# An adaLN block on one Trainium2 core: layer-norm rows of three batches on GpSimd, and one gated product over two PSUM banks

## The chip, the core and the metric

The kernel runs on one core of one Trainium2 chip, on float32 data, in one launch. A core has four engines that compute (TensorE, here PE; VectorE, DVE; ScalarE, ACT; GpSimd, POOL) and SyncE (SP), which issues transfers. Each takes its own instructions in order; they meet by semaphores. The metric is the device time in microseconds (us); less is better.

## What is computed

For x of 4 batches x 1024 rows x 128 columns, with a modulation `mod = silu(c) @ wmod` that gives each batch six vectors (sa, ca, ga, sb, cb, gb):

```python
h = layernorm(x) * (1 + ca) + sa
q, k = l2norm(heads(h @ Wq)), l2norm(heads(h @ Wk)); v = heads(h @ Wv)      # 16 heads of 8
...   # beta, two decays, a per-token gate "flux" from a tiny MLP on k*beta
M_fast, M_slow = einsum(k * beta * w, v * beta) / w.sum()                   # over all 1024 rows
x = x + ga * ((alpha * q @ M_fast + (1 - alpha) * q @ M_slow) @ Wo)
h = layernorm(x) * (1 + cb) + sb
x = x + gb * fp4_linear(silu(fp4_linear(h, w_gate)) * fp4_linear(h, w_up), w_down)   # 352 hidden columns
```

`fp4_linear` rounds activations and weights to a four-bit grid, with one scale for each block of 16 columns, before it multiplies. ga and gb are kept at least 0.25 away from zero.

## The kernel before

The rows of a batch lie as 8 tiles of 128 rows; the unit of work is a pair of tiles, so there are 16 pairs, four to a batch (pair i is of batch i // 4). Everything is fully unrolled. What each engine does in which order is written out by hand in the table ORDER, one list for each engine, of steps like `PP:5` (step PP of pair 5) or `GA:1` (step GA of batch 1); each engine's block walks its list and runs the step's function, if it has one. Waits are on counters whose values follow from these lists. Nothing else sets the order of the work.

Phase one, for each batch. P0 (DVE L797 to L805) takes mean and variance of the 8 tiles, POOL turns the variance into `rstd` with a power (L385). XN makes the normalised tile `xn` = (x - mean) * rstd: for batches 0 and 1 on VectorE (L751, one TENSOR_SCALAR a tile), for batches 2 and 3 on ScalarE (L567, one ACTIVATE a tile, which needs nmr = -mean * rstd, made on POOL, L389). XN_VECTOR = 2 is that border. `xn` has four tiles, two pairs, so XN of pair i waits for the transposes of pair i - 2. PX transposes a pair on TensorE (L1063, L1064) into a bank; ScalarE moves it out as `hT` with the modulation applied (L576). PP multiplies hT by all of the projection weights (L1074, 496 columns a tile); ScalarE copies keys, values and gates to `kvg` (L589) and squares queries and keys to `sq` (L592), and VectorE sums the squares (L810). MB makes the modulation matrices `mb` from wmod (PE, ACT L541), and W0 on VectorE (L779 to L789) brings their gates to the right sign and size.

Then the gate steps of a batch, a long chain over all engines: GA (ACT: table load L512, exp, ln; VectorE's part is zb L824 and, as GB, eg1 L832), GC (POOL adds the logs L405, PE sums them over rows), GD (ACT wexp L624), GS (ACT hmid L633), GE, GF, GY, and V0 to V3 (POOL L424 makes the weighted values, PE L1095 multiplies them with the keys), GG (the memory matrix `wm`). O1, O2 and O3 read the memory for a pair, transpose, and multiply by Wo; O3 on VectorE adds the result to x and takes new statistics. L1 normalises again (ACT L664, POOL L448, L452).

Phase two quantises. A slot s serves the normalised rows of pair s - 4 and the gated FFN rows of pair s - 6 at once, 960 columns: Q (DVE L934 maximum, L939, L942 reciprocal), QR (POOL L461), QA (ACT L675), QT (DVE L950, L953), QO (POOL L473). N4 transposes the first part. F1 multiplies it by the gate and up weights: tile 0's G0 and U0, then tile 1's G1 and U1 (PE L1148, L1150), 352 columns each; G goes to the `pa` banks, U to the `pv` banks. ScalarE makes silu of G0 and G1 to `sgl` (L690), VectorE multiplies each with its U bank into q_x (L964). F3 transposes the quantised products, F4 multiplies by the down weights on top of x, and the pair goes out.

PSUM: three `pa` banks are handed round among all users of that kind (the position in the PE list decides), two `pv` banks among O1, O3 and F1, so a pair's U0 can be in either of the two. `sgl` has two tiles: silu of tile k waits until the product of the pair before has read it.

Transfers are issued by SyncE in this order: x of batch 0 (two halves), the first third of wmod, Wv, three gate weights, x of batch 1, the rest of wmod (L310), five small vectors, Wo, five pieces of the FFN weights, x of batches 2 and 3 (L325). ScalarE issues c, Wtf1, Wk and Wq.

Of the kernel before, what the change touches and what calls it, by code (L numbers as in the profile page):

```python
# [11 lines left out]
P = 128  # L12
# [73 lines left out]
        Q:21 QT:20 QT:21""",
    "tensor": """
        CT:0 RP:0 CM:0 WK:0 WQ:0 PX:0 PX:1 KW:0 PX:2 PP:0 PX:3 PP:1 PX:4 PP:2 PX:5 PP:3 PX:6 MB:0 PX:7 PP:4 PP:5
        PP:6 PX:8 PX:9 GC:0 PX:10 PP:7 PP:8 PP:9 PX:11 GE:0 PP:10 V0:0 V1:0 V2:0 V3:0 PP:11 GG:0 GC:1 O1:0 O1:1
        GE:1 O2:0 PX:12 O2:1 O1:2 O3:0 PX:13 PP:12 O2:2 O3:1 O1:3 V0:1 V1:1 V2:1 V3:1 PX:14 O3:2 O2:3 PP:13 GG:1  # L90
        GC:2 O3:3 W3:0 GE:2 O1:4 O1:5 N4:0 PX:15 PP:14 PP:15 F1:0 O2:4 V0:2 O2:5 O3:4 V1:2 O1:6 V2:2 N4:1 V3:2
        O3:5 F1:1 N4:2 F3:0 F1:2 O2:6 GG:2 F4:0 O3:6 O1:7 GC:3 O1:8 N4:3 F1:3 O2:7 O2:8 GE:3 F3:1 O1:9 N4:4 F1:4
        O3:7 V0:3 O2:9 V1:3 F3:2 O3:8 V2:3 F4:1 N4:5 F1:5 V3:3 F3:3 O1:10 N4:6 O3:9 F4:2 F1:6 F3:4 O2:10 GG:3
        O1:11 O1:12 O3:10 N4:7 O2:11 F4:3 O3:11 F1:7 N4:8 F1:8 F4:4 F3:5 O1:13 O2:12 F3:6 O1:14 O3:12 O2:13 N4:9
        F1:9 O2:14 F4:5 O3:13 F3:7 O3:14 F4:6 N4:10 O1:15 F1:10 N4:11 F1:11 F3:8 O2:15 F4:7 O3:15 F3:9 F4:8
        N4:12 F3:10 F1:12 N4:13 F1:13 F3:11 F4:9 F4:10 F4:11 N4:14 F1:14 N4:15 F1:15 F3:12 F3:13 F4:12 F4:13
# [1109 lines left out]
```

## Time and profile before

| | us |
|---|---|
| three timed runs: median (lowest to highest) | 219.83 (219.64 to 221.18) |
| the profiled execution, by the same clock | 217.84 |
| its span from first to last instruction | 216.0 |
| VectorE / ScalarE / GpSimd busy in the span | 177.0 / 148.3 / 148.0 |
| TensorE matmuls busy | 182.3 |

A time in the trace counts from the start of the span. The profile is of one execution, whose time is the second line; the timed runs are others. Line numbers (L964) are those of the kernel before; names such as `q_x<-sgl,pv` are out<-in; x8 is a number of instructions; "idle before" or square brackets tell how long the engine stood before them and who let it go on.

### The profile page before, as it was taken

The page shows a single profiled execution, that of the slowest core. Times are in us where ns is not written, and L with a number is a line of the kernel's source. Part 1 is how long each engine was busy: PE and PEld are TensorE (multiplying, and loading weights), DVE is VectorE, ACT ScalarE, POOL GpSimd, SP SyncE. Part 2 cuts the span into 40 slices and gives each one's busy share as a digit, 9 for nine tenths or more (in the row PEclk, how much of TensorE's full clock was granted, in tenths as well). Part 3 has the DMA queues.
Part 4 walks back from the last instruction along what each step waited for, and adds up shares of the span by engine and source line. Part 5 has one row for each costly group of instructions (what it writes and reads, how often), then busy time and mean ns, then how long its engine had stood idle before and what let it go on. Part 6 is the DMA issues. An engine that isn't in the chain of part 4 may idle for free. (4 is left out here: it accounts for less than half of the span.)

```text
span 216.0 us, 3457 instructions
## 1 busy us (share of the span) xinstructions
PE 182.3 (84%) x924; PEld 131.0 (61%) x924; DVE 177.0 (82%) x444; ACT 148.3 (69%) x342; POOL 148.0 (68%) x174
## 2 busy tenths in 40 slices
PE   1996935699999989788599999889899898988983
PEld 1642414256767737656375868767688595775863
DVE  3959989756899979899999999998999996876730
ACT  2486997999999997964973656464844557563641
POOL 6334007674879978898978997877858768765540
PEclk9999995999999999999999999999999999999999
DMA  5591000000000000000000010000001000011011
GB/s 163 165 257 35 0 2 0 0 3 0 2 2 0 5 0 0 0 0 5 0 24 0 0 27 26 0 27 3 24 0 49 3 24 24 6 41 32 0 52 49
DMA packets 11500, 5.66 MB, mean 26 GB/s; under 512 B 1685, under 2 KB 11353, under 8 KB 11481
## 3 DMA queue, kind: packets, MB, share of 16 engines
q1 hardware_dynamic: 11168, 5.31, 8.8%
q8 instruction: 8, 0.13, 0.3%
q10 hardware_dynamic: 312, 0.13, 0.2%
q14 instruction: 12, 0.09, 0.1%
HBM read 3.34 MB, written 2.10 MB: 25 GB/s over the span
## 5 line engine op out<-in xcount | busy, mean ns | idle before, releaser
L461 POOL TENSOR_TENSOR q_r<-q_x,q_rs 128x960 f32<-128x960 f32 (+2 forms) x18 | 29.7, 1651 | 13.4 <-DVE q_rs L942 13.4
L473 POOL TENSOR_TENSOR q_o<-q_r,q_sp 128x960 f32<-128x960 f32 (+2 forms) x18 | 29.5, 1641 | 8.8 <-DVE q_r L953 8.3
L1074 PE MATMUL pa<-wcat,hT 128*128 128x496 f32 x64 | 31.3, 615 | 3.0 <-ACT hT L576 1.7
L1148 PE MATMUL pa<-guT,hqT 128*128 128x352 f32 x64 | 25.2, 476 | 5.6 <-ACT hqT L681 5.6
L675 ACT ACTIVATE q_A<-q_r 128x960 f32<-128x960 bf16 (+2 forms) x18 | 16.0, 887 | 16.3 <-POOL q_r L461 11.1
L1171 PE MATMUL pa<-wdg,fqT 128*128 128x128 f32 x192 | 26.7, 275 | 0.0
L690 ACT ACTIVATE sgl<-pa 128x352 f32<-128x352 f32 x32 | 14.6, 462 | 15.5 <-PE pa L1148 12.6
L1150 PE MATMUL pv<-guT,hqT 128*128 128x352 f32 x64 | 24.3, 461 | 0.0
L1171 PEld LDWEIGHTS pa<-wdg,fqT 128*128 128x128 f32 x192 | 24.0, 192 | 0.0
L424 POOL TENSOR_TENSOR vs<-kvg,cw 128x256 f32<-128x256 f32 x32 | 20.0, 649 | 3.8 <-DVE cw L848 3.8
L1074 PEld LDWEIGHTS pa<-wcat,hT 128*128 128x128 f32 x64 | 11.4, 200 | 16.0 <-ACT sq L592 6.0
L950 DVE SCALAR_TENSOR_TENSOR q_x<-q_A,q_r 128x960 f32<-128x960 f32 (+2 forms) x18 | 18.5, 1026 | 2.8 <-ACT q_A L675 2.8
L964 DVE TENSOR_TENSOR q_x<-sgl,pv 128x352 f32<-128x352 f32 x32 | 15.7, 510 | 6.0 <-PE pv L1150 5.5
L934 DVE TENSOR_REDUCE q_am<-q_x 128x60 f32<-128x960 f32 (+2 forms) x18 | 18.7, 1040 | 1.0 <-POOL q_x L452 0.5
L953 DVE SCALAR_TENSOR_TENSOR q_r<-q_A,q_x 128x960 f32<-128x960 f32 (+2 forms) x18 | 18.8, 1046 | 0.6
L1148 PEld LDWEIGHTS pa<-guT,hqT 128*128 128x128 f32 x64 | 11.0, 189 | 11.8 <-ACT hqT L681 7.8
L405 POOL TENSOR_TENSOR lf<-lf 128x224 f32<-128x224 f32 (+2 forms) x12 | 8.2, 680 | 13.3 <-ACT lf L616 12.7
L1150 PEld LDWEIGHTS pv<-guT,hqT 128*128 128x128 f32 x64 | 12.0, 190 | 7.2 <-DVE x_all L905 0.8
L589 ACT ACTIVATE kvg<-pa 128x368 f32<-128x368 f32 x32 | 15.3, 479 | 1.5 <-PE pa L1074 1.3
L1112 PE MATMUL pv<-wm,hT 128*128 128x256 f32 x64 | 16.1, 382 | 0.2 <-DVE x_all L905 0.2
L698 ACT ACTIVATE fqT<-pa 128x384 f32<-128x384 f32 x32 | 14.0, 487 | 3.2 <-PE pa L1159 3.1
L664 ACT ACTIVATE xn<-x_all,nmrb,rstdb 128x128 f32<-128x128 f32 x32 | 14.0, 489 | 2.6 <-DVE nmrb L923 2.6
(151 smaller groups left out, 449.8 us busy)
## 6 DMA issues: line engine op xcount, KB each, us to landing
out_dram<-x_all SPq DMA_DIRECT2D x16, 128.0 KB, 1.8
x_all<-in_L_attn_x_dram SPq DMA_DIRECT2D x3, 512.0 KB, 5.6
x_all<-in_L_attn_x_dram SPq DMA_DIRECT2D x2, 256.0 KB, 3.1
wmod_sb<-in_L_wmod_dram SPq DMA_DIRECT2D x1, 256.0 KB, 4.3
wraw<-in_L_ffn_w_down_dram SPq DMA_DIRECT2D x1, 176.0 KB, 4.2
wmod_sb<-in_L_wmod_dram SPq DMA_DIRECT2D x1, 128.0 KB, 3.8
wraw<-in_L_ffn_w_gate_dram SPq DMA_DIRECT2D x1, 128.0 KB, 3.6
wraw<-in_L_ffn_w_up_dram SPq DMA_DIRECT2D x1, 128.0 KB, 3.1
```

The costliest lines, as they stand in the source:

```text
L424: g.tensor_tensor(vs[:, t].rearrange("p a (h d) -> p a h d", d=DK), vt.unsqueeze(1).to_broadcast([P, 2, H, DK]), cw[:, t].unsqueeze(3).to_ ...
L461: g.tensor_tensor(blocks(q_r[:, s % 2, c]), blocks(q_x[:, s % 2, c]), spread(q_rs[:, s % 2, n]), ALU.mult)\
L473: g.tensor_tensor(blocks(q_o[:, s % 2, c]), blocks(q_r[:, s % 2, c]), spread(q_sp[:, s % 2, n]), ALU.mult)\
L675: a.activation(q_A[:, c], top, ACT.Abs, scale=TOP_SCALE).then_inc(S["q_A"], 1)
L934: v.tensor_reduce(q_am[:, r, n], blocks(q_x[:, r, c]), axis=AX.X, op=ALU.max, apply_absolute_value=True)\
L950: v.scalar_tensor_tensor(q_x[:, r, c], q_A[:, c], MAGIC_FLOOR, q_r[:, r, c], ALU.max, ALU.add)\
L953: v.scalar_tensor_tensor(q_r[:, r, c], q_A[:, c], MAGIC_FLOOR, q_x[:, r, c], ALU.max, ALU.subtract, reverse1=True).then_inc(S["q_q"], 1)
L1074: te.matmul(bank_a(("PP%d" % k, i))[:, 0:NCAT], hT[:, b, 2 * j + k, :], wcat[:, :], start=True, stop=True).then_inc(S["a_full"], 1)
L1112: last = te.matmul(t[:, k * 2 * D:(k + 1) * 2 * D], hT[:, b, 2 * j + k, :], wm[:, b % 2, :], start=True, stop=True)
L1148: te.matmul(bank_a(("G%d" % k, i))[:, 0:I], lhs, guT[:, 0, :], start=True, stop=True)\
L1150: te.matmul(bank_v(("U%d" % k, i))[:, 0:I], lhs, guT[:, 1, :], start=True, stop=True)\
L1171: last = te.matmul(t[:, k * D:(k + 1) * D], fqT[:, (2 * i + k) % 4, ch * P:(ch + 1) * P], wdg[:, b % 2, ch, :], start=False, stop=(ch == 2))
```

## The change

XN moves: batch 0 stays on VectorE, batches 1, 2 and 3 go to GpSimd, as TENSOR_SCALARs with mean and rstd as per-partition scalars; nmr is no longer made. `sgl` becomes two pairs of tiles. The two `pv` banks are one tensor, so that VectorE multiplies both tiles of a pair in one instruction of 2 x 352 columns, after silu of G1 and after U1; it frees both banks at once. TensorE still makes G0, U, G1, U, but which tile's U comes first depends on the bank, so that tile 0 always lies in bank 0. x of batch 2 is issued before the rest of wmod, x of batch 3 last. All four lists of ORDER are written anew.

```diff
-    XN_VECTOR = 2
+    XN_ON = "vggg"
...
-        sgl = sb("sgl", [P, 2, I])
+        sgl = sb("sgl", [P, 2, 2, I])
...
-        pv = [ctx.enter_context(nc.psum_tensor(f"pv{i}", [P, 512], F32)) for i in range(NBANK_V)]
+        pv_all = ctx.enter_context(nc.psum_tensor("pv", [P, NBANK_V, 512], F32))
+        pv = [pv_all[:, k, :] for k in range(NBANK_V)]
...
# SyncE
-            sp.dma_start(wmod_sb[:, 2 * D:6 * D], wmod[:, 2 * D:6 * D]).then_inc(S["wmod"], 16)
...
             sp.dma_start(btf2_b[:, :], btf2.partition_broadcast(P)).then_inc(S["wsm"], 16)
+            sp.dma_start(x_all[:, 2], x_v[2]).then_inc(S["x2"], 16)
+            sp.dma_start(wmod_sb[:, 2 * D:6 * D], wmod[:, 2 * D:6 * D]).then_inc(S["wmod"], 16)
             sp.dma_start(wo_sb[:, :], Wo).then_inc(S["wo"], 16)
...
-            for b in range(2, NB):
-                sp.dma_start(x_all[:, b], x_v[b]).then_inc(S["x%d" % b], 16)
+            sp.dma_start(x_all[:, 3], x_v[3]).then_inc(S["x3"], 16)
# GpSimd
+            def XN(i):
+                b, j = divmod(i, NP_)
+                if XN_ON[b] != "g":
+                    return
+                pool.wait_ge(S["nmean"], stat_count(b, 0))
+                pool.wait_ge(S["rstd"], stat_count(b, 0))
+                if i >= 2:
+                    pool.wait_ge(S["a_full"], slot_a[("XT", i - 2)] + 1)
+                for k in range(2):
+                    t = 2 * j + k
+                    g.tensor_scalar(xn[:, t % 4, :], x_all[:, b, t, :], nmean[:, b, t:t + 1], rstd[:, b, t:t + 1],
+                                    ALU.add, ALU.mult).then_inc(S["xnp"], 1)
# ScalarE, F1
+                if i >= 2:
+                    act.wait_ge(S["v_free"], slot_v[("U1", i - 2)] + 1)
                 for k in range(2):
                     t = bank(("G%d" % k, i))
-                    n = 2 * i + k
-                    if n >= 2:
-                        act.wait_ge(S["v_free"], slot_v[("U%d" % k, i - 1)] + 1)
-                    a.activation(sgl[:, n % 2, :], t[:, 0:I], ACT.Silu).then_inc(S["a_free"], 1)
+                    a.activation(sgl[:, i % 2, k, :], t[:, 0:I], ACT.Silu).then_inc(S["a_free"], 1)
# VectorE, F1
-                for k in range(2):
-                    n = 2 * i + k
-                    t = bank(("U%d" % k, i))
-                    dve.wait_ge(S["a_free"], slot_a[("G%d" % k, i)] + 1)
-                    v.tensor_tensor(q_x[:, r, k * I:(k + 1) * I], sgl[:, n % 2, :], t[:, 0:I], ALU.mult)\
-                        .then_inc(S["v_free"], 1)
+                bank(("U0", i))
+                bank(("U1", i))
+                dve.wait_ge(S["a_free"], slot_a[("G1", i)] + 1)
+                v.tensor_tensor(q_x[:, r, 0:2 * I].rearrange("p (t k) -> p t k", t=2), sgl[:, i % 2], pv_all[:, :, 0:I],
+                                ALU.mult).then_inc(S["v_free"], 2)
# TensorE, F1
+                first = slot_v[("U0", i)] % NBANK_V
...
+                    t = k ^ first
+                    te.matmul(bank_v(("U%d" % k, i))[:, 0:I], hqT[:, i % 2, t * D:(t + 1) * D], guT[:, 1, :],
+                              start=True, stop=True).then_inc(S["v_full"], 1)
```

Of the lists, the stretches around the first gate block. Before and after:

```diff
 scalar
-  ... PX:5 PP:3 PX:6 XN:8 MB:0 PX:7 XN:9 PP:4 PP:5 GA:0 PP:6 PX:8 XN:10 PX:9 W1:0 GD:0 GS:0 PX:10 PP:7 ...
+  ... PP:3 PX:5 MB:0 PX:6 PP:4 WQ:0 PX:7 GA:0 PP:5 PP:6 PX:8 W1:0 PX:9 GD:0 GS:0 PP:7 PP:8 PX:10 ...
 vector
-  ... P0:1 XN:3 XN:4 PP:0 XN:5 XN:6 P0:2 PP:1 PP:2 XN:7 GA:0 PP:3 P0:3 W0:0 GB:0 ...
+  ... XN:3 P0:1 PP:0 P0:2 PP:1 PP:2 GA:0 PP:3 P0:3 W0:0 GB:0 ...
 gpsimd
-  P0:0 P0:1 P0:2 KC:0 GC:0 GB:0 V0:0 V1:0 P0:3 V2:0 GF:0 V3:0 GC:1 ...
+  P0:0 P0:1 XN:4 XN:5 XN:6 P0:2 KC:0 XN:7 P0:3 GO:0 XN:8 XN:9 GC:0 GB:0 XN:10 GO:1 V0:0 XN:11 V1:0 V2:0 V3:0 XN:12 GF:0 GC:1 GB:1 W2:0 XN:13 XN:14 ...
```

From F1:0 on the lists hold the same steps as before with small exchanges of neighbours.

## Rows read from the trace of the kernel before

**Rows 1.** Busy time by stage: length, PE, PEld, DVE, ACT, POOL busy, granted clock, DMA.

```profile
0.00:20.00 20.00, 13.46 (x42) 7.54 (x43) 13.66 (x79) 10.85 (x29) 8.33 (x17) 1.00 0.62 168
20.00:41.00 21.00, 14.06 (x36) 6.68 (x35) 18.56 (x46) 19.24 (x43) 7.38 (x16) 0.84 0.00 0
41.00:82.00 41.00, 38.78 (x163) 26.01 (x164) 33.11 (x93) 39.93 (x106) 32.40 (x48) 1.00 0.01 1
82.00:180.00 98.00, 86.76 (x503) 67.81 (x501) 91.95 (x200) 61.19 (x130) 81.32 (x82) 1.00 0.04 12
180.00:216.00 36.00, 29.22 (x186) 22.91 (x183) 19.77 (x30) 17.05 (x39) 18.55 (x15) 1.00 0.11 31
```

**Rows 2.** Waits (us in total, times, longest), TensorE 41 to 82, ScalarE 20 to 82.

```profile
PE pa L1074 <- ACT hT L576: 1.7, 1, 1.7
...
ACT wexp L624 <- PE pg L1083: 1.2, 1, 1.2
```

**Rows 3.** Groups by line: ScalarE's XN in all, in 41 to 82 us, VectorE's XN.

```profile
L567 ACT ACTIVATE xn<-x_all,nmr,rstd 128x128 f32<-128x128 f32 x16 | 7.0, 496 | 0.2 <-POOL nmr L389 0.2
...
L567 ACT ACTIVATE xn<-x_all,nmr,rstd 128x128 f32<-128x128 f32 x10 | 4.4, 496 | 0.0
...
L751 DVE TENSOR_SCALAR xn<-x_all,nmean,rstd 128x128 f32<-128x128 f32 x16 | 4.6, 341 | 1.3 <-issue 1.3
```

**Rows 4.** Groups by line, GpSimd.

```profile
L385 POOL TENSOR_TENSOR rstd<-ve,mhalf 128x8 f32<-128x8 f32 x3 | 5.2, 1722 | 9.4 <-DVE ve L804 9.4
...
L434 POOL TENSOR_TENSOR wog<-wo_sb,mb 128x128 f32<-128x128 f32 x4 | 1.8, 460 | 0.0
...
L357 POOL TENSOR_SCALAR w_s<-w_sp 128x70 f32<-128x70 f32 x1 | 0.3, 261 | 0.1
```

**Rows 5.** Timeline (start, us): SyncE's issues, VectorE and ScalarE at batch 2's arrival.

```profile
4.73 0.58 SPq L310 DMA_DIRECT2D wmod_sb<-in_L_wmod_dram  x1
...
10.65 1.36 SPq L325 DMA_DIRECT2D x_all<-in_L_attn_x_dram  x2
...
16.22 1.64 DVE L797 BATCH_NORM_STATS2 st<-x_all 128x6 f32<-128x128 f32 x8 [1.31 <-DMA x_all<-in_L_attn_x_dram]
...
19.31 0.38 ACT L592 ACTIVATE sq<-pa 128x256 f32<-128x256 f32 x1 [1.70 <-DVE ss L810]
```

**Rows 6.** Timeline from 28 to 34 us: VectorE, then ScalarE behind GA:0.

```profile
28.41 0.69 DVE L789 SCALAR_TENSOR_TENSOR mb<-mb_sgn,mb 128x512 f32<-128x512 f32 x1
29.80 0.36 DVE L832 TENSOR_SCALAR eg<-eg 128x384 f32<-128x384 f32 x1 [0.70 <-ACT eg L601]
...
32.03 0.46 ACT L589 ACTIVATE kvg<-pa 128x368 f32<-128x368 f32 x1
...
33.27 0.59 ACT L576 ACTIVATE hT<-pa,colmod 128x256 f32<-128x256 f32 x1
```

**Rows 7.** Timeline, VectorE: the gated products and a 704-column operation.

```profile
117.30 0.52 DVE L964 TENSOR_TENSOR q_x<-sgl,pv 128x352 f32<-128x352 f32 x1 [0.30 <-PE pv L1150]
...
145.13 0.95 DVE L964 TENSOR_TENSOR q_x<-sgl,pv 128x352 f32<-128x352 f32 x2
146.12 1.15 DVE L934 TENSOR_REDUCE q_am<-q_x 128x60 f32<-128x960 f32 x1
...
200.80 0.52 DVE L964 TENSOR_TENSOR q_x<-sgl,pv 128x352 f32<-128x352 f32 x1 [0.61 <-PE pv L1150]
...
202.84 0.83 DVE L950 SCALAR_TENSOR_TENSOR q_x<-q_A,q_r 128x704 f32<-128x704 f32 x1
203.70 0.89 DVE L953 SCALAR_TENSOR_TENSOR q_r<-q_A,q_x 128x704 f32<-128x704 f32 x1
```

**Rows 8.** VectorE's coefficient row: duration ns minimum/median/maximum.

```profile
L877 DVE SCALAR_TENSOR_TENSOR coef<-yt,rn x4: 279/284/1229, 49.7 to 132.8; 128x128 f32<-128x128 f32 x4
```

**Rows 9.** The chain that ended last (start, us, what), two of its pieces.

```profile
172.80 0.53 DVE q_x L964
...
203.01 1.38 POOL q_r L461
```

More of the change, by code:

```diff
@@ L87 @@
[L87 to L96 removed]
+        P0:0 P0:1 XN:4 XN:5 XN:6 P0:2 KC:0 XN:7 P0:3 GO:0 XN:8 XN:9 GC:0 GB:0 XN:10 GO:1 V0:0 XN:11 V1:0 V2:0
@@ new lines @@
+        QR:19 QO:18 QO:19 GH:3 QR:20 QR:21 QO:20 QO:21""",
+    "scalar": """
+        CT:0 CM:0 WK:0 PX:0 PX:1 PX:2 KW:0 PX:3 PP:0 PP:1 PP:2 PX:4 PP:3 PX:5 MB:0 PX:6 PP:4 WQ:0 PX:7 GA:0 PP:5
+        PP:6 PX:8 W1:0 PX:9 GD:0 GS:0 PP:7 PP:8 PX:10 GE:0 PP:9 PX:11 GA:1 PP:10 PP:11 GG:0 GD:1 GS:1 O2:0 PX:12
+        O2:1 PP:12 O2:2 GE:1 GA:2 L1:0 PX:13 O2:3 PX:14 L1:1 PP:13 GD:2 W3:0 QA:4 GG:1 GS:2 N4:0 QA:5 PX:15
+        PP:14 L1:2 PP:15 F1:0 L1:3 O2:4 O2:5 GA:3 QA:6 N4:1 F1:1 GE:2 L1:4 N4:2 F1:2 GS:3 O2:6 QA:7 GG:2 F3:0
+        GD:3 QA:8 F4:0 L1:5 N4:3 F1:3 O2:7 O2:8 L1:6 F3:1 N4:4 F1:4 GE:3 QA:9 F3:2 QA:10 F4:1 O2:9 N4:5 L1:7
+        F1:5 F3:3 N4:6 QA:11 L1:8 F1:6 F4:2 O2:10 GG:3 F3:4 QA:12 L1:9 O2:11 N4:7 F4:3 L1:10 F1:7 N4:8 F1:8 F3:5
+        O2:12 QA:13 F3:6 QA:14 F4:4 O2:13 N4:9 L1:11 F1:9 O2:14 L1:12 F4:5 QA:15 N4:10 F4:6 F3:7 L1:13 F1:10
+        N4:11 F1:11 O2:15 QA:16 F4:7 F3:8 QA:17 F3:9 F4:8 L1:14 N4:12 F1:12 N4:13 L1:15 F1:13 F3:10 QA:18 F4:9
+        F3:11 QA:19 F4:10 F4:11 N4:14 F1:14 N4:15 F1:15 F3:12 QA:20 F3:13 F4:12 QA:21 F4:13 F3:14 F4:14 F3:15
+        F4:15""",
@@ L265, in adaln_block_kernel @@
                 "xn2", "u", "wdg", "c", "wqk", "w1", "btf2h", "w_r", "w_A", "xn", "col", "zb", "kvg", "ss",
-                "eg1", "eg", "lnss", "rn", "lg", "hz", "al0", "yt", "nmrb", "bias0", "scB", "xn0", "w_rs",
+                "eg1", "eg", "lnss", "rn", "lg", "hz", "al0", "yt", "nmrb", "bias0", "scB", "xn0", "xnp", "w_rs",
                 "w_t", "bn", "mv", "nmean", "cf", "rt", "rt1", "mrt", "sfx", "coef", "bnb", "mvb", "eps", "h2", "w_sp", "x1",
@@ L290, in stat_count, with xn_nth @@
             return k + 1 if b == 0 else b + 2
+        def xn_nth(i):
+            return sum(1 for k in range(i + 1) if XN_ON[k // NP_] == XN_ON[i // NP_])
         def gates(b, lo, hi):
@@ L483, in GH @@
                                 ALU.mult).then_inc(S["wdg"], 1)
-            run = {"KC": KC, "W2": W2, "W3": W3, "P0": P0, "GB": GB, "GC": GC, "GF": GF, "GO": GO, "GH": GH, "O3": O3, "L1": L1,
+            run = {"KC": KC, "XN": XN, "W2": W2, "W3": W3, "P0": P0, "GB": GB, "GC": GC, "GF": GF, "GO": GO, "GH": GH, "O3": O3, "L1": L1,
                    "QR": QR, "QO": QO}
@@ L559, in XN @@
                 b, j = divmod(i, NP_)
-                if b < XN_VECTOR:
+                if XN_ON[b] != "a":
                     return
-                act.wait_ge(S["nmr"], b - XN_VECTOR + 1)
+                act.wait_ge(S["nmr"], XN_ON[:b + 1].count("a"))
                 if i >= 2:
@@ L742, in XN @@
                 b, j = divmod(i, NP_)
-                if b >= XN_VECTOR:
+                if XN_ON[b] != "v":
                     return
```

61 lines of the change are left out of this document (26 added, 35 removed).

## Prediction

> **What bounds the kernel now.** I read the busy time by stage first. From 20 to 82 us ScalarE (ACT) has hardly a free moment (59.2 of 62 us; in 41 to 82 us 39.9 of 41), with TensorE just below it in the second part (38.8 of 41). From 82 to 180 us VectorE is the full engine (92.0 of 98), GpSimd (POOL) has 81.3 and ACT only 61.2. In the last 36 us nobody is full: quantise, transpose and multiply of the last pairs follow each other [rows 1]. The waits say the same: between 41 and 82 us TensorE's projection waits for ScalarE to turn a transposed tile into hT (the longest wait 1.7 us), while ScalarE's own longest wait between 20 and 82 us is 1.2 us, for the sum over the decays [rows 2]. So up to the first FFN product (F1:0, at the border of these stages, 82 us) the time is ScalarE's, behind it VectorE's, and the end is a chain.
>
> **Part 1: the layer-norm rows of batches 1 to 3 go to GpSimd.** ScalarE loses 16 ACTIVATEs of 496 ns, which occupy it for 7.0 us because neighbours overlap; 10 of them, 4.4 us, lie between 41 and 82 us and the other six, 2.6 us, before. VectorE loses 8 of its 16 rows, half of 4.6 us = 2.3 us [rows 3]. GpSimd gets 24 TENSOR_SCALARs 128x128 with one tensor input and two per-partition scalars. The trace has no such row. The nearest from below is a TENSOR_SCALAR 128x70 of 261 ns, from above a two-input TENSOR_TENSOR 128x128 of 460 ns, and very far off the 8-element power, 1722 ns, whose cost is its function and not its length [rows 4]. I take 0.35 us, nearer to the one-input row: 24 x 0.35 = 8.4 us (6.3 to 11.0 by the two near ends, 41 by the far one). GpSimd has 11.7 + 13.6 = 25.3 us free before 41 us and 8.6 us in 41 to 82 [rows 1]; some 14 of the 24 run in the first part and 10 in the second (3.5 us), so at 0.35 us they hide under its own idle time. Without that cover each would delay GpSimd's next step by its length. The Trainium skill ("GPSIMD Engine Reference", section Engine selection) says that one-input work on GpSimd runs at roughly line rate and two-input work at half of VectorE's; by its cycle figure 128 elements take about 0.11 us beside the dispatch, an estimate that would put the row at the lower end; the 261 ns row, one-input too, agrees in kind, and no row here has the two scalars.
>
> **Part 2: transfers.** x of batch 2 is issued at 10.65 us, behind the rest of wmod, wo and five FFN weight transfers. VectorE, which takes its queue in order, stood 1.31 us for it at 16.2 us; the sum of squares behind it came late, and ScalarE stood 1.70 us for that at 19.3 us [rows 5]. Twelve issues lie between 4.73 us (wmod) and 10.65 us, 0.49 us each [rows 5]. In the new order seven of those ahead of it come behind, so batch 2 is issued and lands some 3.4 us earlier and the stall goes: -1.7 us. What could be late next: wmod is issued 2.9 us later, at about 7.7 us, but its matrices (MB) are made only after the stalled ScalarE step of 19.3 us, so it is not; batch 3 comes last as before and is read after batch 2's and four pairs' work.
>
> **What it gives by stage.** The first gate block of batch 0 (GA:0) does not become free by what ScalarE loses: in the middle of it, eg1 on VectorE runs at 29.80 us behind the modulation's sign steps, whose last starts at 28.41 and takes 0.69 us [rows 6], and these wait for the matrices. It moves by the 1.7 us of the stall. From there to 41 us ScalarE loses the pair XN:10 (2 x 0.44 = 0.9 us) and, since work is moved in ahead of the decay step, its 1.2 us of waiting [rows 2], and gets the pair PP:5 that stood ahead of GA:0 (33.27 - 32.03 = 1.24 us) [rows 6]: -0.9. That makes -2.6 us at 41 us. TensorE has only 14.1 of 21 us of work there and a mean granted clock of 0.84, part of the stretch at the lower level of 1.2 GHz, against 1.00 after it [rows 1]; GA:0 still blocks ScalarE in the same way, so I leave that as it is. From 41 to 82 us ScalarE would give 4.4 us, but TensorE has only 41.0 - 38.8 = 2.2 us to lose [rows 1], and three rotating banks will not close all of it. I take 1.5 us, between 0 and 4.4. So F1:0 comes 4.1 us earlier. VectorE behind it is as full as before with the same list of work, so the shift is kept to the end; the 2.3 us of its own rows lie before 21 us, where it is busy 13.7 of 20 us anyway [rows 1].
>
> **Part 3: one product for two tiles.** Two instructions of 352 columns, back to back, keep VectorE for 146.12 - 145.13 = 0.99 us. For 704 columns with one operand in PSUM the nearest is L950 to L953 at the end, 203.70 - 202.84 = 0.86 us. So a pair whose inputs are all there gains 0.13 us. But where VectorE waits for the second up-projection it is the other way: before, 0.52 us were left once U1 had ended (start 117.30), now the whole 0.88 us start there: +0.36. Such a second product with a gap of its own, 0.3 to 0.6 us, appears seven times in 16, first at 117.30 and last at 200.80 [rows 7]. All in all 9 x -0.13 + 7 x 0.36 = +1.3 us if each counted. The chain that ended last passes the product of 172.80 (late one), and ends over q_r at 203.01 [rows 9], which waits for the reciprocal behind the product of 200.80 (late one); a third product on it is back to back. That is 2 x 0.36 - 0.13 = +0.6 us, which I take; ends -16 x 0.13 = -2.1 and 7 x 0.36 = +2.5. Both banks now come free together, half a microsecond later for the first; TensorE's next user of it stands behind other matmuls mostly, so I add nothing. The silu rows get a full second buffer and lose no time. The Trainium skill ("VectorE: DVE Perf Modes", Rules for kernel authors) advises fewer VectorE operations since each pays its start; its figure of about 150 cycles (156 ns) would give 16 x 0.156 = -2.5 us as an estimate. The rows show 0.13 instead, and only where nothing is awaited.
>
> **Sum.** -2.6 - 1.5 + 0.6 = -3.5 us. Against the profiled execution (217.84 us, span 216.0) that is 214.3; the median of the three timed runs is 2.0 us higher, 219.83, so the forecast for it is **216.3 us**. The new written order on every engine can move each of these terms by a microsecond.
>
> **Rivals.**
> A. ScalarE alone was the limit, TensorE only looked full because its rows follow ScalarE's pace: the full 7.0 us and the 1.7 us stall come back, with no loss in the product: 219.8 - 8.7 = 211.1 us. For it: ScalarE's 1.1 us of idle in 41 us. Against: TensorE has 2.2 us of idle there, and its matmuls do not get shorter.
> B. TensorE holds the second stage and the late products all count: -2.6 + 0 + 2.5 = -0.1: 219.7 us, no change. For it: the 38.8 of 41 us and the seven gaps. Against: most gaps lie where VectorE is not on the chain.
> C. Slower. GpSimd's queue is in order, and each XN waits there for a transpose two pairs earlier, with GC, V and QR behind it. Its room in 41 to 82 us is 8.6 us; ten rows fill it at 0.86 us each, and from there every further tenth costs 1 us. At the far end (1.72 us) it is 17.2 - 8.6 = +8.6 us, less the 2.6 of before: 219.8 + 6.0 = 225.8 us. For it: per-partition scalars on GpSimd are not in the trace. Against: the 261 ns row. Waits for the transposes work alike: XN:8 also stands behind GO:0, which waits for the sign steps ending at 29.1 us.
> D. The two engines get in each other's way. A coefficient row on VectorE takes 279 ns at least and 1229 at most [rows 8], so something now and then holds it for 0.95 us. If half of the 24 new rows hold a VectorE step for their own 0.35 us while it is full (18.6 of 21 us, [rows 1]), that costs 4.2 us, of which the idle time hides half: 216.3 + 2.1 = 218.4 us. The Trainium skill ("SBUF — State Buffer", Who interferes with whom) says that GpSimd and a VectorE operation with two SBUF inputs exclude each other for a whole instruction; by that rule the spread of that row is such a lock, and the trace agrees in that it occurs.
>
> **How the numbers follow.** Forecast 0.45, A 0.20, B 0.15, C 0.10, D 0.10. A measurement of this kernel tells about 1% from no change, 2.2 us, so faster means below 217.6. Of the forecast's 0.45 (its own range 213.5 to 218.5) 0.39 lies below that, all of A, and a little of D: 0.61. B, most of D and the rest of the forecast: 0.27. C and the tail of B: 0.12. The range reaches from A (211.1) to beyond B: 211.0 to 220.6, leaving out most of C and a little at the low end.
>
> **What the profile after would show.** GpSimd's new row at 0.3 to 0.45 us, 24 times; no ACTIVATE from x_all and nmr; no wait for x at 16 us; eg1 of batch 0 near 28.1; the first gated product 4 us earlier than before; ScalarE below 37 of 41 us in the second stage with TensorE at 38 or more; one product of 0.85 to 0.9 us, 16 times; VectorE's stage from F1:0 to the tail as long as before or up to 1 us longer. I am wrong if the row costs over 0.8 us, if F1:0 moves by 7 us or not at all, or if the stretch behind F1:0 changes by more than 2 us.

## The result, and the profile after

The changed kernel takes 223.09 us (median, 221.1 to 224.57) against 219.85 us for the kernel before in the same rounds: a ratio of 1.013, 95% interval [1.0095, 1.0165]. It is slower by 1.3%, 2.1 to 3.6 us. The medians are of all executions, while the ratio leaves out those that were over 1.5% above the fastest of their kernel (four of the ten after, near 224.5 us). The profiled execution took 221.18 us (span 219.4); for the kernel before those were 217.84 and 216.0. Single profiles are read here for where time goes, the ratios for how much.

Busy time by stage of the kernel after, same columns as in [rows 1] (the last stage ends at 219.4):

```profile
0.00:20.00 20.00, 14.67 (x39) 7.78 (x40) 12.03 (x73) 10.52 (x27) 10.79 (x23) 1.00 0.62 168
20.00:41.00 21.00, 16.11 (x43) 7.42 (x42) 19.52 (x46) 19.15 (x42) 15.20 (x26) 0.92 0.00 1
41.00:82.00 41.00, 39.08 (x170) 26.67 (x170) 34.29 (x93) 37.62 (x95) 36.57 (x58) 1.00 0.00 1
82.00:180.00 98.00, 86.32 (x488) 66.89 (x487) 87.43 (x179) 57.65 (x122) 76.83 (x78) 0.98 0.04 12
```

Up to 82 us the picture is near the predicted one: from 41 us on ScalarE has 37.6 of 41 us where it had 39.9 (I had said below 37), TensorE is at 39.1, and GpSimd works 26.0 of the first 41 us where it worked 15.7: the new rows lie in what was its idle time. From 82 us on VectorE, the engine that was full before (92.0 of 98), is busy only 87.4: it now waits. The product's group before, then after (line, engine, operation, count | busy us, mean ns | idle before and who ended it):

```profile
L964 DVE TENSOR_TENSOR q_x<-sgl,pv 128x352 f32<-128x352 f32 x32 | 15.7, 510 | 6.0 <-PE pv L1150 5.5 <-issue 0.3
```

```profile
L980 DVE TENSOR_TENSOR q_x<-sgl,pv 128x704 f32<-128x704 f32 x16 | 14.1, 884 | 12.2 <-PE pv L1164 11.1
```

The new rows on GpSimd, first as a group, then with the minimum, median and maximum duration in ns:

```profile
L406 POOL TENSOR_SCALAR xn<-x_all,nmean,rstd 128x128 f32<-128x128 f32 x24 | 12.2, 516 | 2.8 <-DVE nmean L822 2.5 <-issue 0.2 <-PE pa L1077 0.2
```

```profile
L406 POOL TENSOR_SCALAR xn<-x_all,nmean,rstd x24: 441/447/1582, 13.6 to 72.8; 128x128 f32<-128x128 f32 x24
```

The product's group had 6.0 us of idle ahead of it before and has 12.2 now. The new GpSimd row takes 447 ns in the median, where I had taken 0.35 us. Some rows take longer, so the mean is 516 ns and the whole step 12.2 us, beyond the upper of my two near ends (6.3 to 11.0). The longest, 1.58 us, is the second of a pair, beside a row of VectorE with 1120 columns and two inputs in SBUF:

```profile
35.33 2.01 POOL L406 TENSOR_SCALAR xn<-x_all,nmean,rstd 128x128 f32<-128x128 f32 x2
```

```profile
35.76 1.34 DVE L787 SCALAR_TENSOR_TENSOR wraw<-w_A,w_r 128x1120 f32<-128x1120 bf16 x1 [0.79 <-ACT w_A L563]
```

So the two engines seem to have got in each other's way here too, at the rows where rival D had looked.

Where the time went is best read by single events that both kernels have. The starts of the first silu of F1:0 on ScalarE, before and after:

```profile
81.85 0.47 ACT L690 ACTIVATE sgl<-pa 128x352 f32<-128x352 f32 x1
```

```profile
79.72 0.52 ACT L707 ACTIVATE sgl<-pa 128x352 f32<-128x352 f32 x1
```

So F1:0 comes 2.1 us earlier, not 4.1. The end of the first product moves by less, 84.5 to 83.0. The ends of the gated products of pairs 0 to 15, taken off VectorE's timeline of each kernel (us; the experiments are explained below):

| kernel | 0 | 1 | 2 | 3 | 4 | 5 | 9 | 12 | 15 |
|---|---|---|---|---|---|---|---|---|---|
| before | 84.5 | 94.8 | 99.5 | 112.7 | 117.8 | 128.2 | 160.0 | 184.0 | 201.3 |
| after | 83.0 | 93.5 | 99.8 | 112.0 | 118.2 | 129.0 | 161.8 | 186.8 | 204.7 |
| after, exchange undone (n13) | 82.4 | 92.9 | 97.3 | 109.9 | 115.6 | 126.4 | 159.1 | 184.2 | 202.1 |
| after, split products (m2) | 84.9 | 95.2 | 101.6 | 114.0 | 119.2 | 131.5 | 163.2 | 187.2 | 205.1 |
| both undone (n14) | 83.2 | 93.5 | 98.1 | 110.6 | 115.7 | 126.4 | 158.2 | 182.1 | 200.0 |
| best (m6) | 82.5 | 92.8 | 97.5 | 110.7 | 115.8 | 126.2 | 158.0 | 182.0 | 199.3 |
| best with merged product (m11) | 81.8 | 92.4 | 97.5 | 112.4 | 118.2 | 129.4 | 162.2 | 187.3 | 204.9 |
| best with the exchange (n16) | 82.1 | 92.4 | 98.8 | 111.0 | 116.1 | 126.5 | 158.3 | 182.3 | 199.6 |

Each row is one execution, with its own stretches at the lower clock: m2's has one from 40 to 48 us (mean granted clock 0.78), where n14's has none, and m2 is 1.7 us later from product 0 on. Differences within a row say more than those between rows.

Two losses show behind the earlier start. One is sudden: from product 1 to product 2 the kernel after takes 6.3 us where before took 4.7, and its lead of 1.3 us is gone (it has 0.7 of it once more at product 3, and is behind from product 4 on). The other is a drift: from product 4 to 15 it takes 86.5 us where before took 83.5.

The sudden one can be seen in the timelines. The kernel before, then after (start, duration, engine, line, operation):

```profile
98.07 0.53 DVE L942 RECIPROCAL q_rs<-q_sp 128x60 f32<-128x60 f32 x1
98.52 0.10 DVE L923 SCALAR_TENSOR_TENSOR nmrb<-mvb,rstdb 128x2 f32<-128x2 f32 x1
98.53 0.94 DVE L964 TENSOR_TENSOR q_x<-sgl,pv 128x352 f32<-128x352 f32 x2
...
98.68 1.82 POOL L461 TENSOR_TENSOR q_r<-q_x,q_rs 128x960 f32<-128x960 f32 x1 [0.86 <-DVE q_rs L942]
```

```profile
96.60 0.53 DVE L959 RECIPROCAL q_rs<-q_sp 128x60 f32<-128x60 f32 x1
97.04 0.36 DVE L902 TENSOR_TENSOR mbd<-pg,mrt 128x256 f32<-128x256 f32 x1
97.32 1.72 DVE L940 SCALAR_TENSOR_TENSOR nmrb<-mvb,rstdb 128x2 f32<-128x2 f32 x1
98.97 0.87 DVE L980 TENSOR_TENSOR q_x<-sgl,pv 128x704 f32<-128x704 f32 x1
...
97.20 1.82 POOL L479 TENSOR_TENSOR q_r<-q_x,q_rs 128x960 f32<-128x960 f32 x1 [0.69 <-DVE q_rs L959]
```

nmrb has two elements a partition and takes 0.10 us before and 1.72 us after. It ends at 99.04, and GpSimd's q_r at 99.02. Both engines wait for the same reciprocal. Before, nmrb follows the reciprocal at once and starts 0.16 us ahead of q_r; after, one of the "small exchanges of neighbours" (`GG:2 Q:7` has become `Q:7 GG:2`) has put the mbd row of GG:2, 0.36 us, between them, nmrb starts 0.12 us behind q_r and stays until q_r is done. And it is on the chain that ended last (pieces in order of time, the kernel after):

```profile
97.05 0.05 DVE mbd L902
97.10 0.22 issue
97.32 1.72 DVE nmrb L940
99.05 0.81 DVE q_x L980
99.85 0.14 issue
99.99 2.04 PE pv L1125 x4
```

The four matmuls behind it take 2.04 us; in the kernel with the exchange undone (n13, below) the same four take 1.10. TensorE had stood 1.83 us for this product, whose bank they need, and its granted clock was at the lower level in part of the next stretch (windows of the kernel after, columns as in [rows 1]):

```profile
96.00:100.00 4.00, 1.75 (x10) 0.88 (x8) 3.93 (x6) 3.33 (x8) 3.23 (x4) 0.95 0.00 0
100.00:104.00 4.00, 4.00 (x16) 3.48 (x17) 3.90 (x6) 1.32 (x4) 2.59 (x3) 0.62 0.00 0
```

A mean of 0.62 over 4 us, between levels 1.0 and 0.5, is about 3 us at 1.2 GHz. The Trainium skill ("SBUF — State Buffer", Who interferes with whom) says that GpSimd and a VectorE operation with two SBUF inputs shut each other out for a whole instruction. The trace agrees: the held row reads mvb and rstdb, both in SBUF. In the kernel before, the products behind nmrb, each with one operand in PSUM, took their usual 0.94 us for two beside the running q_r (98.68 to 100.50).

### The profile page after: what moved, and what is told of

It reads as the page before. It is cut to its first block, busy times and chain, and to the rows that moved or that the text cites. A ratio compares the mean times of both kernels' runs of the same rounds, so it can differ in the third digit from the quotient of the medians.

```text
span 219.4 us, 3421 instructions
## 1 busy us (share of the span) xinstructions
PE 186.3 (85%) x924; PEld 132.3 (60%) x924; DVE 175.4 (80%) x420; ACT 144.4 (66%) x326; POOL 160.3 (73%) x196
## 4 chain that ended last, share of the span: by engine, by line
PE 31%; DVE 18%; POOL 17%; ACT 16%; issue 16%; DMA 1%; DVEq 0%; POOLq 0%; ACTq 0%
PE pa L1087 6%; POOL q_r L479 5%; PE pa L1161 5%; POOL q_o L491 4%; PE pv L1164 4%; ACT L530 4%; PE pa L1185 3%; ACT hmid L651 2%; DVE q_x L967 2%; DVE q_x L980 2%; POOL q_x L466 2%; DVE hz L873 2%; PE pv L1125 2%; PE pa L1173 2%; DVE ss L827 2%
## 5 line engine op out<-in xcount | busy, mean ns | idle before, releaser
L479 POOL TENSOR_TENSOR q_r<-q_x,q_rs 128x960 f32<-128x960 f32 (+2 forms) x18 | 29.7, 1651 | 17.2 <-DVE q_rs L959 16.3
L1087 PE MATMUL pa<-wcat,hT 128*128 128x496 f32 x64 | 33.0, 641 | 5.3 <-ACT sq L610 5.1
L980 DVE TENSOR_TENSOR q_x<-sgl,pv 128x704 f32<-128x704 f32 x16 | 14.1, 884 | 12.2 <-PE pv L1164 11.1
L1087 PEld LDWEIGHTS pa<-wcat,hT 128*128 128x128 f32 x64 | 12.0, 206 | 18.2 <-ACT sq L610 9.1
L1125 PE MATMUL pv<-wm,hT 128*128 128x256 f32 x64 | 17.5, 402 | 2.3 <-DVE q_x L980 1.8
L466 POOL TENSOR_TENSOR q_x<-xn,mb 128x256 f32<-128x256 f32 x16 | 11.6, 726 | 6.6 <-issue 6.6
L1108 PE MATMUL pg<-vs,kvg 128*128 128x256 f32 x64 | 15.9, 381 | 0.6 <-DVE ws L878 0.6
```

The costliest lines, as they stand in the source:

```text
L479: g.tensor_tensor(blocks(q_r[:, s % 2, c]), blocks(q_x[:, s % 2, c]), spread(q_rs[:, s % 2, n]), ALU.mult)\
L980: v.tensor_tensor(q_x[:, r, 0:2 * I].rearrange("p (t k) -> p t k", t=2), sgl[:, i % 2], pv_all[:, :, 0:I], ALU.mult).then_inc(S["v_free"], 2)
L1087: te.matmul(bank_a(("PP%d" % k, i))[:, 0:NCAT], hT[:, b, 2 * j + k, :], wcat[:, :], start=True, stop=True).then_inc(S["a_full"], 1)
L1125: last = te.matmul(t[:, k * 2 * D:(k + 1) * 2 * D], hT[:, b, 2 * j + k, :], wm[:, b % 2, :], start=True, stop=True)
```

## The experiments

Sixteen kernels ran. "Lists" are those of ORDER; a head is a list up to F1:0 (on GpSimd up to QR:6), a tail what follows. Ratios are to the kernel before, run in the same rounds (its medians 219.15 to 219.42).

**First the two parts apart.** m1 is the kernel before with the merged product alone, m2 the kernel after with two products again (the five places of the F1 diff, each taken over or back). m3 is the kernel before with the GpSimd rows alone: its own transfers and lists, the new XN steps put into GpSimd's list. m4 is m1's late start without its merged instruction: two products, each freeing its own bank, behind one common wait for both up-projections and silu of G1.

```diff
# m1: before, F1 as in the change        # m2: after, F1 as before
# m3, gpsimd list
-  P0:0 P0:1 P0:2 KC:0 GC:0 GB:0 V0:0 V1:0 P0:3 ...
+  P0:0 P0:1 XN:4 XN:5 XN:6 P0:2 KC:0 XN:7 XN:8 XN:9 GC:0 GB:0 XN:10 XN:11 V0:0 V1:0 P0:3 XN:12 ...
# m4, before, VectorE's F1
+                ts = [bank(("U%d" % k, i)) for k in range(2)]
+                dve.wait_ge(S["a_free"], slot_a[("G1", i)] + 1)
                 for k in range(2):
-                    t = bank(("U%d" % k, i))
-                    dve.wait_ge(S["a_free"], slot_a[("G%d" % k, i)] + 1)
```

> The kernel before with the one product over two banks alone (silu buffer of two pairs and TensorE's order of the up-projections with it); the lists, the rows and the transfers are those of before. Theory M (the joined product is what costs: VectorE stands at the head of its queue until the last of the four matmuls has ended, and then has 0.88 us to do instead of 0.5): idle time before the product goes from 6 to about 12 us and the time is 3 to 5 us above before, 223 to 225 us. Theory O (the product is harmless, and what was lost behind 82 us comes from the new lists): 219 to 221 us.

Measured: 224.39 us, ratio 1.0242 [1.0171, 1.0312].

> The changed kernel with the product split again into two, one a tile, and the silu buffer of two tiles; lists, GpSimd rows and transfers as in the changed kernel. Theory M: 217.5 to 219 us, 1.5 us or a little more below before, the gain that stood at the first product. Theory O: still above 221 us.

Measured: 220.29 us, ratio 1.0051 [1.001, 1.0093].

> The kernel before with the rows of batches 1 to 3 on GpSimd alone: before's lists, with the 12 GpSimd steps set into its list, before's transfers, split products. Theory T (TensorE limits the stretch from 41 to 82 us, so taking 7 us from ScalarE gives little): 217 to 219 us. Theory S (ScalarE was the limit and the new lists or transfers ate the gain): 213 to 215 us. A third way, GpSimd's 24 rows of 0.45 us and their waits hold its queue: above 220.5 us.

Measured: 223.07 us, ratio 1.0177 [1.0106, 1.0249]; the first product ends at 88.3 us where before it was 84.5.

> The kernel before with the two products kept apart, each giving its bank back on its own, but both started only when G1 and U1 are there. Theory M1 (it is the late start with the whole work still to do): as the joined product alone, some 0.1 us a pair worse, 3.5 to 6 us above before, 223.5 to 226 us. Theory M2 (it is the two banks given back at once, for which TensorE waits): near before, within 1.5 us, 219 to 221.5 us.

Measured: 224.09 us, ratio 1.0207 [1.0121, 1.0293]. Product groups of m1, then of m4:

```profile
L963 DVE TENSOR_TENSOR q_x<-sgl,pv 128x704 f32<-128x704 f32 x16 | 14.2, 887 | 13.6 <-PE pv L1150 12.9 <-ACT sgl L690 0.5
```

```profile
L964 DVE TENSOR_TENSOR q_x<-sgl,pv 128x352 f32<-128x352 f32 x32 | 15.1, 514 | 10.3 <-PE pv L1150 9.6 <-ACT sgl L690 0.5
```

The merged product costs 5.2 us in the lists of before (m1), and in those of after 2.8 by the medians and 1.7 by the ratios (m2 to the kernel after). Two separate products that merely start late cost nearly as much as m1: 4.9 us by the medians, 4.5 by the ratios. The difference, 0.3 to 0.8 us, lies within the intervals. So the bulk is neither the instruction nor the common release of the banks. It is that the first half no longer runs while TensorE makes G1 and U1 and ScalarE silu of G1. m3 shows that the rows on GpSimd are no gain by themselves, put in among its old steps. It is 3.9 us slower, and the first product is already 3.8 us late. The loss does not come at the start: the table load of GA:0 is 0.4 us late (28.38 for 27.95), that of GA:1 2.8 us (49.97 for 47.16). Between them four of the new rows take 4.12 us, beside VectorE's two rows of 1120 columns (from 36.62 to 39.74), and TensorE waits for them:

```profile
37.06 4.12 POOL L405 TENSOR_SCALAR xn<-x_all,nmean,rstd 128x128 f32<-128x128 f32 x4
40.37 0.47 PE L1077 MATMUL pa<-ident,xn 128*128 128x128 f32 x1 [2.71 <-POOL xn L405]
```

But m2 stays slower than before although its first stage is the improved one: something else in the lists costs.

**Then head and tail.** m5 has the rows, transfers and heads of after, split products and the tails of before. m6 is m5 with the start of before (VectorE: `MV:0 SB:0` ahead of `XN:2`; TensorE and ScalarE: `KW:0` ahead of `PX:2`, `PP:0` ahead of `PX:3`; TensorE also `CT:0` ahead of `RP:0`). m7 is the kernel before with the tails of after alone. m8 is m5 with the rows taken back from GpSimd, their steps set into the lists of VectorE and ScalarE at places like those of before (those lists are not among the lines below).

```diff
# m6 against m5, vector, then scalar
-  P0:0 XN:0 XN:1 XN:2 SB:0 MV:0 XN:3 ...
+  P0:0 XN:0 XN:1 MV:0 SB:0 XN:2 XN:3 ...
-  CT:0 CM:0 WK:0 PX:0 PX:1 PX:2 KW:0 PX:3 PP:0 PP:1 ...
+  CT:0 CM:0 WK:0 PX:0 PX:1 KW:0 PX:2 PP:0 PX:3 PP:1 ...
# m8 against m5
-    XN_ON = "vggg"
+    XN_ON = "vvaa"
```

> Split products; rows on GpSimd, new transfers and new lists up to the first FFN product (F1:0, on GpSimd up to QR:6); behind it the lists of before. Theory L (the exchanges of neighbours behind F1:0 lose what the first part gained): 217.5 to 218.5 us, 1 to 2 us below before. Theory N (the gain of the first part is not there, or TensorE's clock takes it back): as the changed kernel with split products, 219.5 to 220.5 us.

Measured: 217.4 us, ratio 0.9904 [0.9861, 0.9946].

> As m5, and up to the first projection TensorE, ScalarE and VectorE take their steps in the order of before again (the small tables MV and KW earlier). In the changed kernel ScalarE's first kvg came at 12.2 us instead of 11.1. If the start counts: 1 us below m5. If what follows evens it out: as m5.

Measured: 215.99 us, ratio 0.9848 [0.9809, 0.9888], the fastest of all and faster than both kernels.

> The kernel before with nothing changed but the order behind F1:0, which is that of the changed kernel; split products. Theory L: 221 to 222.5 us. Theory N: within 0.7 us of before.

Measured: 221.93 us, ratio 1.0125 [1.0068, 1.0182].

> As m5, but the rows back on VectorE (batch 1) and ScalarE (batches 2 and 3), set into these lists at places like those of before; transfers as in the changed kernel. The theory that the rows on GpSimd do give something but TensorE takes most of it: 1 to 2.5 us above m5. That they give nothing: as m5. The full 7 us of ScalarE: 5 us or more above m5.

Measured: 221.49 us, ratio 1.0081 [1.0034, 1.0129].

So the step from VectorE and ScalarE to GpSimd is worth 4.1 us (m8 to m5) once the heads are made for it. The stages of m8 and of m5 from 20 to 82 us show what it does:

```profile
20.00:41.00 21.00, 16.52 (x41) 7.81 (x39) 18.19 (x45) 19.23 (x43) 9.16 (x16) 0.84 0.00 0
41.00:82.00 41.00, 37.53 (x158) 25.34 (x159) 33.31 (x90) 39.85 (x104) 29.97 (x44) 1.00 0.01 1
```

```profile
20.00:41.00 21.00, 16.10 (x43) 7.44 (x41) 19.47 (x46) 19.16 (x42) 15.21 (x26) 0.92 0.00 1
41.00:82.00 41.00, 39.06 (x169) 26.63 (x169) 34.23 (x93) 37.70 (x95) 36.55 (x57) 1.00 0.00 1
```

ScalarE goes from 39.9 to 37.7 of 41 us and TensorE gets 11 more matmuls done in the stage. The mean granted clock of 20 to 41 us also differs, 0.84 and 0.92, and its share is not separated here. The new start costs 1.4 us by the medians (m5 to m6, 1.2 by the ratios, whose intervals overlap): the first copy to kvg on ScalarE is at 12.2 us in the kernel after and at 11.2 in m6, and VectorE then waits 2.85 us for sq, 2.21 in m6. At the first silu of F1:0 0.65 us of it are left (79.80 in m5, 79.15 in m6). And the tails, which I had called the same steps, cost 2.6 us alone (m7).

**Which exchange?** The two-element row pointed to `Q:7 GG:2`. m9 puts that exchange alone into the kernel before; m10 takes it alone out of m7. (The expectations call nmrb a row of GG:2; it is L1:5's. GG:2's row is mbd, which the exchange puts ahead of it.) In the same rounds, two terms of the sum were priced in the best version: m11 is m6 with the merged product, m12 is m6 with the transfers of before.

```diff
# m9 against before, vector
-  F1:1 GY:2 GG:2 Q:7 L1:5 F1:2
+  F1:1 GY:2 Q:7 GG:2 L1:5 F1:2
# m10 against m7: the same, the other way
```

> The kernel before with one exchange in VectorE's list: the quantise reduction of pair 1 (Q:7) ahead of the gated nmr of pair 2's neighbour (GG:2), as after has it. Lock theory: the two-element row that makes nmrb (0.10 us before) now starts while GpSimd's quantise row of 1.82 us runs, and lasts until that has ended, 1.5 us and more; the end of product 2 moves from 99.5 to about 101.5 us and the kernel takes 1.0 to 2.0 us more than before, 220.3 to 221.2 us. Rival (order of TensorE and ScalarE is what costs, VectorE's exchange is a matter of 0.1 us): no change, 219.3 us, nmrb 0.10 us.

Measured: 219.42 us, ratio 1.0018 [0.9974, 1.0061]. nmrb takes 1.72 us and product 2 ends at 101.4 as expected; but the time does not follow.

> The kernel before with after's order behind F1:0, but with GG:2 ahead of Q:7 on VectorE as before. Lock theory: nmrb falls from 1.72 us to about 0.1, product 2 ends near 99.8 us rather than at 101.7, and the kernel is 1.2 to 2 us faster than with all of after's order behind F1:0 (221.9): about 220.3 us. Rival (the other exchanges cost): 221.5 to 222 us.

Measured: 218.44 us, ratio 0.9951 [0.9903, 1.0]: undone in m7's lists, the same exchange gives 3.8 us (1.0125 to 0.9951).

> The best version so far (rows on GpSimd, new transfers, after's lists up to F1:0 but with before's start, before's lists behind, split products; 216.0 us) with the merged product alone added. Late-start theory: each product starts only when the second up-projection is there, VectorE's idle ahead of it rises by some 7 us and the cost is 3 to 5 us as it was in the lists of before (+5.2): 219 to 221 us. Rival (the cost came from the particular lists, and a freer first stage pays for it): 216.0 to 217.5 us.

Measured: 221.49 us, ratio 1.0078 [1.0038, 1.0118].

> The same best version (216.0 us) with the transfers in the order of before: wmod ahead of the small ones, x of batch 2 behind the FFN weights. Stall theory of the prediction: VectorE or GpSimd waits for batch 2 near 16 us again and F1:0 comes about 1.7 us later: 217.7 us. Rival (the rows of batch 2 are GpSimd's now and late ones in its list, so the transfer is hidden): 215.8 to 216.3 us.

Measured: 218.58 us, ratio 1.0004 [0.9958, 1.005].

m11 against m6: +5.0 us by the ratios, 5.5 by the medians. The product groups, m6 and m11:

```profile
L981 DVE TENSOR_TENSOR q_x<-sgl,pv 128x352 f32<-128x352 f32 x32 | 15.6, 511 | 5.8 <-PE pv L1164 5.7
```

```profile
L980 DVE TENSOR_TENSOR q_x<-sgl,pv 128x704 f32<-128x704 f32 x16 | 14.2, 884 | 11.4 <-PE pv L1164 10.8 <-ACT sgl L707 0.5
```

1.4 us less work, 5.6 us more waiting. In m6 the two products of pair 9 run back to back at 157.07 with nothing before them; in m11 the merged one stands 0.51 us for U1:

```profile
157.07 0.95 DVE L981 TENSOR_TENSOR q_x<-sgl,pv 128x352 f32<-128x352 f32 x2
```

```profile
161.31 0.89 DVE L980 TENSOR_TENSOR q_x<-sgl,pv 128x704 f32<-128x704 f32 x1 [0.51 <-PE pv L1164]
```

From product 4 to 15, m6 takes 83.5 us and m11 86.7. Another 3.1 us come between products 0 and 4, and 1.7 of it between 2 and 3, where m11 has a stretch at the lower clock (0.57 in 100 to 104 us, behind one in which TensorE worked 2.19 of 4 us) and m6 has none. The transfers are worth 2.6 us by the medians and 3.4 by the ratios (m12 to m6). In m12 VectorE stands 2.23 us for x at 16.3 us and the first product is 1.4 us late, about the stall that I had priced at 1.7; the rest appears between products 2 and 4 (19.8 us, m6 18.3), with a granted clock of 0.61 in 108 to 112 us.

**The exchange in the kernels that matter.** n13 is the kernel after with the one exchange undone, n14 the same with split products, n15 is m6 with n14's tails, n16 is m6 with the exchange put in.

```diff
# n13 against after, n14 against m2, vector
-  F1:1 GY:2 Q:7 GG:2 L1:5 F1:2
+  F1:1 GY:2 GG:2 Q:7 L1:5 F1:2
# n16 against m6: the other way
```

> The kernel after, with one exchange of VectorE's list undone: GG:2 (nmrb of batch 2, a row of two elements) ahead of Q:7 again. Exchange theory (the whole +2.6 to +2.9 us of the new lists behind F1:0 hangs on this one exchange, as two of my runs with the lists of before ahead of F1:0 say): nmrb 0.10 us in place of 1.72, product 2 ends near 98.1 rather than 99.8, 223.1 becomes 219.5 to 221 us, a ratio to before of 0.997 to 1.008. Rival (with the exchange alone in before's lists nothing measurable was lost, so its cost is taken up further down): 222.5 to 223.5 us, ratio 1.011 to 1.017.

Measured: 219.51 us, ratio 1.0031 [0.9988, 1.0074].

> The kernel after with two products in place of the merged one (220.3 us) and the same exchange undone. Exchange theory: 217.4 to 218.0 us, as the version with before's lists behind F1:0 (217.4). Rival: 219.8 to 220.5 us.

Measured: 218.26 us, ratio 0.9929 [0.9881, 0.9976].

> The best version so far (216.0 us) with after's lists behind F1:0 and the exchange undone. If those lists without the exchange are as good as before's: 215.5 to 216.5 us. If the gain seen with them in the lists of before (ratio 0.995) is real: about 215 us.

Measured: 216.29 us, ratio 0.989 [0.9795, 0.9985].

> The best version so far (216.0 us) with the exchange alone put in (Q:7 ahead of GG:2 on VectorE). Lock theory: nmrb starts behind GpSimd's row of 1.82 us and ends with it, product 2 is 1.7 us later; if the later stages take up half of it, as they did in the lists of before, 216.5 to 217.5 us; if TensorE falls to its lower level in the hole as well, 217.5 to 218.5. Rival (harmless here): 215.8 to 216.3 us, nmrb 0.10 us.

Measured: 216.9 us, ratio 0.987 [0.9794, 0.9945].

In the kernel after, moving one step of 0.36 us back by one place gives 2.2 us by the ratios (3.6 by the medians). n13's timeline at that place, and its window of the next stretch:

```profile
96.00 0.53 DVE L959 RECIPROCAL q_rs<-q_sp 128x60 f32<-128x60 f32 x1
96.45 0.10 DVE L940 SCALAR_TENSOR_TENSOR nmrb<-mvb,rstdb 128x2 f32<-128x2 f32 x1
96.46 0.88 DVE L980 TENSOR_TENSOR q_x<-sgl,pv 128x704 f32<-128x704 f32 x1
```

```profile
100.00:104.00 4.00, 3.68 (x27) 3.58 (x28) 3.90 (x10) 3.07 (x6) 4.00 (x4) 1.00 0.01 2
```

With split products it is 2.7 us (m2 to n14), in m7 3.8, both by the ratios; in the tails of before it is 0.4 (m9) and 0.5 (n16), neither told from nothing. The rest of the new tails costs nothing that can be told (m6 to n15, +0.3 us by the medians, +0.9 by the ratios, intervals overlapping).

Why one and the same 1.7 us counts in the tails of after and not in those of before: from product 1 to 2 it takes 6.3 or 6.4 us in the kernels of the table that have the exchange and 4.4 to 5.1 in those that have not. But in the tails of before 1.0 us of it is regained by product 3 (m6 13.2 us from 2 to 3, n16 12.2), in those of after hardly any (n14 12.5, m2 12.4). TensorE's timeline suggests the reason. In m2 and in m7 it has O1:7 two short steps behind the up-projection, into the bank that the product has not freed; m7:

```profile
101.40 1.14 PE L1112 MATMUL pv<-wm,hT 128*128 128x256 f32 x4 [1.47 <-DVE q_x L964]
```

In the tails of before, F4:0 and O3:6 stand ahead of O1:7, and in n16 TensorE does not wait for that product. Part of what is regained looks like a hold as well: the three hz rows on VectorE (L873) take 2.21 us in m6 and 1.69 in n16, where GpSimd's rows lie elsewhere. That the order of TensorE's list is what decides is read from the waits, and was not tried by itself. In m2 and m7 a second loss follows, from product 4 to 5: 12.3 us, where n14 and m10 take 10.7 and 10.8. Those two profiles have the lower clock in part of 124 to 132 us, the kernel after does not, and takes 10.8 us there, as n13 does. So m2 to n14 and m7 to m10 may hold some 1.5 us of the clock that the step from after to n13 does not.

## Why the prediction was wrong, by its own steps

The forecast was 216.3 us (-3.5), range 211.0 to 220.6, the result 223.09 (+3.2 by the medians, +2.9 by the ratio). From -3.5 to +2.9 are 6.4 us: the head gave 2.1 us where I had 4.1 (2.0), the merged product cost 1.7 where I had 0.6 (1.1), one exchange cost 2.7 where I had nothing, and the remaining 0.6 are the rest of the tails, which no run tells from nothing.

- **"From 20 to 82 us ScalarE, then VectorE, then a chain": right in kind.** Work taken from ScalarE brings F1:0 forward (83.06 in m8, 79.80 in m5), and work or waiting put on VectorE behind it comes out in the time (m1, m4).
- **Part 1, rows on GpSimd: right in kind.** The row costs 0.447 us in the median and 0.516 in the mean, not 0.35, and in the new lists still hides. Of the 4.1 us that I gave the head, 1.7 were the stall, so the rows had 2.4; measured are 4.1 (m8 to m5). But m8's lists are made for the rows on GpSimd and slow without them, and in lists not made for it the same step loses 3.9 us (m3). The rows have no worth apart from their order, and my terms treated them as if they had.
- **Part 2, transfers: right.** A stall of 1.7 us gone; measured 2.6 us by the medians in m12 (3.4 by the ratios), 1.4 of it at the first product.
- **"-2.6 us at 41 us, -1.5 to 82": too large by 2.0 us.** The table load of GA:0 came 1.4 us earlier (27.95 to 26.53), GS:0 1.2 (38.98 to 37.81), F1:0 2.1. So the 0.9 us between the gate block and 41 us did not come, and the stretch behind gave 0.9 and not 1.5. What I left out is the new start (`XN:2` and `PX:2` ahead of `MV:0`, `KW:0`), never priced: with the old one (m6) GA:0 comes 2.5 us earlier and F1:0 2.7. That is 0.6 of the missing 2.0 us. The other 1.4 were lost behind GA:0, and no run shows to what.
- **Part 3, merged product: mis-sized, by how many of the late starts count.** "+0.36 us where VectorE waits for the second up-projection" is about what the rows show: 5.6 us more of waiting over 16 products, 0.35 each. But I let it count in two places ("2 x 0.36 - 0.13 = +0.6", upper bound +2.5). VectorE's list is full behind F1:0, and each 0.3 us is passed on: +3.2 us from product 4 to 15 in the best lists (m6 to m11), +2.2 in those of after with the exchange undone (n14 84.3, n13 86.5), and a total by the ratios of 1.7 (m2 to after) or 2.2 (n14 to n13) to 5.3 us (m1). I took the pairs without a gap for safe, since VectorE came to them late; but in m11 pairs 1, 5, 9 and 13, without any gap in m6, have one of 0.22, 1.09, 0.51 and 0.46 us. The rule of the Trainium skill ("VectorE: DVE Perf Modes", Rules for kernel authors) to keep the number of VectorE operations small, with that page's fixed term of about 150 cycles for each, would have given an estimated -2.5 us. The trace does not bear that out: the busy time fell by 1.4 us (m6 to m11), and the time rose.
- **"The new written order on every engine can move each of these terms by a microsecond": the step that failed most.** I gave the order no price, and one exchange of neighbours costs 2.2 us in the kernel after (n13 to after). Its mechanism stood in rival D, and its row in [rows 8], as something that "now and then holds" VectorE for 0.95 us; I looked for it at the new GpSimd rows and took the old pairings of VectorE and GpSimd rows for fixed. They are set by what each engine does first behind the same reciprocal, and an exchange changes that.
- **The sum again, with measured terms:** the kernel after with both faults undone is n14, ratio 0.9929, -1.6 us; the exchange adds 2.7 (m2: 1.0051); the merged product adds 1.7 (after: 1.013). Together +2.8, measured +2.9 by the ratio. (These are steps from one kernel to the next, so they add up whatever they are; each by itself is what was measured.) The rivals: A and C (GpSimd's queue too full) did not happen in the kernel after. B had the late products all count, D had the two engines in each other's way, and each had only one part of it; none had a gain in the head together with losses in the tail.

By the signs that I had named: "the stretch behind F1:0 changes by more than 2 us" did come true. From F1:0's first silu to the end of the last product it was 119.5 us (201.3 - 81.85) and is 125.0 (204.7 - 79.72).

Open: how much of each difference is the lower clock. Executions of the kernel before with a mean granted clock of 0.984 took 218.2 us (median of 19), those with 0.976 219.4 (26): by this, an estimate, one stretch more costs some 1 us. Right behind the hole that the exchange opens in TensorE's work such a stretch follows in the profiles of after and m7, but not in those of m2, m9 and n16; a single profile for each can't say how often. The exchange costs something without it too. Among executions with a mean clock of 0.984 or 0.985 the kernel after took 221.1 to 222.2 us and n13 219.4 to 220.9, m2 219.3 to 219.6 and n14 217.9 to 218.5.
